# Gathers that wait for TensorE: a limit of eight groups from the thirteenth group of tiles on

## The reference

```
h = silu(einsum('td,efd->tef', x, w1))
h_mean = einsum('tef,te->ef', h, mask) / max(counts, 1)
y_mean = einsum('ef,edf->ed', h_mean, w2)
out = einsum('tk,tkd->td', routing_w, y_mean[top_idx])
```

## Time and profile before

| | us |
|---|---|
| timed runs, median of 3 | 421.34 (420.61 to 424.37) |
| profiled execution, span from first to last instruction | 501.4 |
| PE busy in the profiled execution | 397.6 |
| VectorE busy | 311.4 |
| ScalarE busy | 218.1 |
| GpSimd busy | 205.3 |

### The profile page before, as it was taken

The page is one execution under the profiler, slowest core; times in us unless marked ns, Lnnn a source line. Parts: engine busy times, 40 slices in busy tenths (PEclk is TensorE's granted clock), DMA queues, the critical chain, the costliest instruction groups (busy, mean ns, idle before and its releaser), DMA issues.

```text
span 501.4 us, 7310 instructions
## 1 busy us (share of the span) xinstructions
PE 397.6 (79%) x1929; PEld 269.9 (54%) x1930; DVE 311.4 (62%) x827; ACT 218.1 (43%) x423; POOL 205.3 (41%) x231
## 2 busy tenths in 40 slices
PE   8999999998898987554591404589987877899984
PEld 7888888886898974423440101244433433344552
DVE  3598888888788999543530101577744543577884
ACT  3334555445232666536350101456644443567320
POOL 2011111115400998757467775400066666610510
PEclk9999999998998996756587556799999788999998
DMA  6206533322209350647312111100291111100029
GB/s 182 66 1 164 139 86 109 102 80 82 81 1 262 98 140 2 193 140 212 106 57 52 54 52 43 31 0 2 54 331 47 37 47 42 47 16 1 1 73 251
DMA packets 53020, 43.68 MB, mean 87 GB/s; under 512 B 20686, under 2 KB 45980, under 8 KB 52732
## 3 DMA queue, kind: packets, MB, share of 16 engines
q1 hardware_dynamic: 44276, 32.09, 22.3%
q0 software_dynamic: 4416, 9.05, 6.5%
q10 hardware_dynamic: 4296, 2.15, 1.6%
HBM read 34.86 MB, written 8.42 MB: 86 GB/s over the span
## 4 chain that ended last, share of the span: by engine, by line
PE 47%; DVE 19%; issue 12%; another core or an unknown queue 10%; ACT 6%; POOL 3%; DVEq 2%; ACTq 0%; POOLq 0%
PE P L662 16%; PE P L935 14%; PE P L867 6%; ACT P L1265 4%; DVE BIG L1712 3%; DVE H L1828 2%; PE P L905 2%; PE P L1062 2%; PE P L697 2%; PE P L655 1%; POOL XN L597 1%; DVE arena L1504 1%; POOL arena L594 1%; PE P L688 1%
## 5 line engine op out<-in xcount | busy, mean ns | idle before, releaser
L1712 DVE TENSOR_TENSOR BIG<-BIG,P 128x512 f32 x138 | 95.0, 688 | 115.9 <-issue 75.1
L935 PE MATMUL P<-w1T,arena 128*128 x276 | 142.4, 652 | 12.0 <-DVE BIG L1712 8.7
L935 PEld LDWEIGHTS P<-w1T,arena 128*128 128x128 f32 x276 | 52.6, 209 | 67.1 <-issue 66.4
L1254 ACT COPY arena<-P 128x384 f32<-128x384 f32 (+1 forms) x48 | 22.4, 467 | 119.6 <-remote 50.4
L1265 ACT ACTIVATE P<-P 128x512 f32<-128x512 f32 x138 | 72.8, 580 | 1.6 <-PE P L935 1.5
L614 POOL DMA_INDIRECT XN<-table,arena x60 | 58.1, 968 | 30.1 <-issue 18.1
L614 POOL DMA_INDIRECT arena<-table,arena x42 | 39.7, 946 | 57.9 <-PE P L935 40.8
L557 POOL TENSOR_TENSOR rs<-ve,mhalf 123x4 f32<-123x4 f32 x16 | 17.6, 1098 | 101.9 <-DVE ve L1356 101.9
L1103 ACT ACTIVATE arena<-P 128x492 f32<-128x492 f32 x48 | 27.9, 583 | 50.6 <-PE P L662 50.5
L614 POOL DMA_INDIRECT BIG<-table,arena x36 | 34.6, 960 | 24.7 <-remote 12.4
L905 PE MATMUL P<-ident,XN 128*128 128x128 f32 x60 | 11.4, 304 | 41.6 <-issue 35.3
(11 more groups left out here) (242 smaller groups left out, 639.7 us busy)
## 6 DMA issues: line engine op xcount, KB each, us to landing
arena<-kpad SPq DMA_DIRECT2D x16, 492.0 KB, 4.0
XN<-in_L_ffn_w SPq DMA_DIRECT2D x1, 4096.0 KB
arena<-in_x SPq DMA_DIRECT2D x16, 224.0 KB
table<-XN SPq DMA_DIRECT2D x4, 896.0 KB
BIG<-table SPq DMA_DIRECT2D x1, 2048.0 KB
out<-H SPq DMA_DIRECT2D x8, 224.0 KB
out<-H ACTq DMA_DIRECT2D x8, 224.0 KB
BIG<-table SPq DMA_DIRECT2D x1, 1024.0 KB
```

The costliest lines, as they stand in the source:

```text
L935: mm = nc.tensor.matmul(bank[:, :], stat, w1T[:, bass.ds(e * FF, FF)], start=True, stop=True)
L1254: nc.scalar.copy(GTs[:, bank, 0:count * SLOT], PT[:, 0:count * SLOT]).then_inc(GT_ready, 1)
L1712: v.tensor_tensor(at, at, bank[:, :], ALU.add).then_inc(esum_step, 1)
```

## The change

A constant FREE_GROUPS = 12 takes the place of EARLY_GROUPS in the loop that issues the gathers. Groups 0 to 11 (tiles 0 to 35) do not wait for `group_mm`. Every group from the thirteenth on, g = 12 and up, waits until `group_mm` is at least g - 7, so until the transposes of group g - 8 are done. For groups 12 to 19 this wait is new; for groups 20 to 27 it takes the place of a wait for the group 20 before; for groups 28 and up it is the wait that they had. Buffers, indices, table, the other waits and all other engines stay as they are.

```diff
 EARLY_GROUPS = UNROLLED // GG
+FREE_GROUPS = 12
...
             for g, (first, count) in enumerate(GROUPS):
-                if g >= EARLY_GROUPS:
-                    pool.wait_ge(group_mm, g - (GSLOTS if g >= EARLY_GROUPS + GSLOTS else EARLY_GROUPS) + 1)
+                if g >= FREE_GROUPS:
+                    pool.wait_ge(group_mm, g - GSLOTS + 1)
                 for n in range(first, first + count):
```

## The result

The changed kernel takes 423.33 us (median of 11 runs, 422.90 to 426.46) against 421.58 us for the kernel before in the same series. The ratio is 1.005 [1.0031, 1.007], so the change costs 2.1 us [1.3, 3.0]: a real loss, and within the 1% that was called no change.

What follows compares the result with a forecast made beforehand. In a stage without stops, TensorE's products set the end, with GpSimd's slower gathers 2.4 us ahead. A 6.4 us stop makes rows 4.0 us late, less 1.7 given back: 421.3 + 2.3 = 423.6 us, range 419.5 to 428.0.

Steps and rivals of the forecast that it cites:

- The stops: Engine standstills in the first profile, 97.0 us in all; at most 16.9 us of them can be in a timed run.
- The sum: Rows 4.0 us late at the end, less 1.7 us given back: 2.3 us added to 421.3, giving 423.6 us.
- One stop, then a slide: GpSimd stands still 6.4 us before tile 36, group 12's first gather; the whole gather stream then slides by that.
- Later waits never last: After group 12 the count is always up before GpSimd needs it; closest at group 18, 285.4 against 286.1 us.
- The detour: TensorE's transposes of the routing weights at tiles 23 to 26, taken to add 4.4 us to the products.
- Who ends last before: Before the change the products set the end, tile 137's rows being there 2.4 us ahead of TensorE.
- The tail: After the last transposes, a last tile alone needs 3.1 us instead of 4.8, giving 1.7 us back.
- The landing: Time from a gather's issue until its rows arrive, taken as 2.8 us, with 1.7 kept for the range.
- The clock: TensorE's short late waits, up to 0.85 us a group from about group 36, cost no granted clock: nothing taken.
- Faster: Rival: free gathers stop the engines in timed runs too; pacing them removes 8.8 us, giving 412.5 us; chance 0.09.
- No effect: Rival: the gathers never come onto the path, so the time stays at 421.3 us; chance 0.21.
- Slower: Rival: gathers held by three wide VectorE operations lose 3.7 us, total gain in time 5.5, 426.8 us; chance 0.24.

Runs made afterwards that it cites:

- e1: The kernel before, unchanged, run again for a second profile: 421.35 us, ratio 0.9999, profiled span 419.6 us.
- e2: The kernel before with the new limit of eight groups at group 12 only: 423.52 us, ratio 1.0045.
- e3: The changed kernel with a limit of ten groups instead of eight for groups 12 to 27: 421.36 us, ratio 1.0003.
- e4: The changed kernel with a limit of six groups instead of eight for groups 12 to 27: 430.75 us, ratio 1.0232.
- e5: The kernel before with the second transposes of the routing weights behind tile 31 instead of tile 26: 421.30 us, ratio 1.0001.
- e7: The kernel before without the three gathers of group 9, whose transposes take group 0's rows: 418.21 us, ratio 0.9931.
- e10: The changed kernel with VectorE's 123x1024 operations beside gathers (one-hots, two products and sum of the weights) in quarters: 424.58 us, ratio 1.0071.
- e12: The changed kernel with only the two products and the sum of the weights on VectorE in quarters: 423.51 us, ratio 1.0053.
- e9: The kernel before with VectorE's 123x1024 operations beside gathers (one-hots, two products and sum of the weights) in quarters: 420.23 us, ratio 0.9968.

## Why the prediction was right, and where its sum was wrong

**The stops.** Right: they are in none of the later profiles. The sum had left up to 16.9 us of them in a timed run; in fact it had taken away too much. Tile 9's products come 14.4 us earlier in e1 (248.14 for 262.54), not 24.0, and from there to the last addition's end e1 takes 136.7 us (to 379.23 + 5.61), not 132.0. Between e1's span and its own time, 421.30, lie 1.7 us; the 9 to 15 us that the Trainium skill, "Runtime: NRT & Kernel Launch", section on the ~15µs preamble/postamble breakdown, gives for what surrounds a kernel are not seen here.

**One stop, then a slide.** Right as a mechanism: e2 gives the time with one wait, e3 and e4 move the stop and the time moves with it. The size was wrong, 2.4 us (and 0.5 at group 18) for 6.4. The first step that failed is the gap between tile 36 and tile 9's products, which I read as 257.21 against 262.54, 5.3 us; in e1 it is 247.02 against 248.14, 1.1 us. The disturbed execution had stretched it at both ends. TensorE's timeline in that first profile of the kernel before:

```profile
251.30 0.52 PE L905 MATMUL P<-ident,XN 128*128 128x128 f32 x3
252.03 4.53 PE L935 MATMUL P<-w1T,arena 128*128 x6 [0.21 <-issue]
```

There the first six products took 4.53 us, at a granted clock of 0.61 (252.03 to 256.40); undisturbed they take 2.84, at 1.00: 1.7 us. And tile 32 was issued 0.2 us after the first product (252.21 against 252.03), when GpSimd had stood 3.02 us there for the routing's last products on TensorE; undisturbed it comes 2.7 us after the first product (242.10 against 239.40), because GpSimd arrives later than these and does not stand: 2.5 us. Together 4.2, the difference between 5.3 and 1.1.

**Later waits never last.** Nearly right. I put group 18's count at 285.4 for a gather at 286.1. The detour was costed at 4.4 us; undisturbed, tiles 21 to 30 take 15.35 us (259.83 to 275.18) for three groups that are worth 8.72, 6.6 us more. That turns the margin of 0.7 us into 1.5 too little; the two gathers held for 1.1 us in between take most of it back, and what is left is the stop at tile 54, 0.5 us.

**Who ends last before.** Wrong: I had the rows 2.4 us ahead of the products. e1's chain, e5 and e7 show the stream ending last, with 2.4 us of TensorE's time lost to it. Two steps failed. One is the error above in another place: tile 36 comes 4.2 us later against TensorE than I read it. The longer detour (2.2 us) and the quicker landing give more than half of that back, so that at tile 137, the one that I compared, the rows would still be ahead by some 1.1 us: in e1 they land at about 376.5 (374.10 and the 2.4 of tile 134), and at e7's pace TensorE would have reached its transposes at 377.6 (e7: 247.45, tile 9's products, to 376.94; e1: from 248.14). The other step is the choice of tile 137. The wait that sets the end is that of group 44, tiles 132 to 134, three gathers earlier: from its transposes TensorE has 7.0 us of work up to those of tile 137 (369.97 to 376.94 in e7), GpSimd only 3.75. Its rows landed at 372.76 in e1, and at e7's pace TensorE would have stood there at 370.66: 2.1 us behind, not ahead.

**The tail.** Wrong too, and for the same reason: the last tile is never alone, so nothing is given back. VectorE's last additions in the changed kernel:

```profile
382.39 5.61 DVE L1713 TENSOR_TENSOR BIG<-BIG,P 128x512 f32 x7 [0.22 <-DVE BIG L1713]
```

They end at 388.00, 4.8 us after the transposes of tile 137 at 383.18, whose rows had landed by about 379.7. It is the same 4.8 us in e1 (380.02 to 384.84) and e7 (376.94 to 381.75), where the products set the end. The forecast's 3.1, and the 1.7 us that it was to save, are in no run.

**The sum.** 6.4 - 2.4 - 1.7 = 2.3 was forecast; 2.9 in the profiles' spans and 2.1 [1.3, 3.0] in the runs was measured. In the same terms the stops are 2.4 + 0.5 instead of 6.4, the lead is none instead of 2.4, and the short tail gives none instead of 1.7. That the total came out has two reasons. The wrong place of tile 36 makes the stop and the lead too long alike and drops out of their difference as long as there is a lead. The rest is luck: by the pace of the products the rows cost 5.5 us after the change and not 4.0, none of which comes back instead of 1.7, and 2.4 us of the 5.5 had been lost before the change already, where I had none.

**The landing.** Taken as 2.8, from a row of another transfer; this line on the gathers of the changed kernel shows 2.5:

```profile
DMA to landing us min/median/max: 2.4/2.5/7.8
```

**The clock.** Right to take nothing for the late waits: the granted clock is 1.00 where they lie. The changed kernel's windows over the expert stage and over its last 23 us (length, busy us by engine, then the granted clock):

```profile
239.40:387.40 148.00, 141.90 (x434) 67.94 (x434) 99.04 (x146) 92.56 (x191) 103.00 (x108) 0.99 0.24 78
...
357.00:380.00 23.00, 20.62 (x58) 8.97 (x59) 12.75 (x19) 12.21 (x26) 16.04 (x17) 1.00 0.17 52
```

It fell elsewhere: between 262 and 268 us, after TensorE had stood 0.42 and 1.25 us for VectorE at the detour, it was 0.72, in the changed kernel and in e1 alike. That is part of the detour's 6.6 us and no price of the change.

**The rivals.** Faster falls: there are no stops to take away, and the changed kernel is slower. No effect falls: 1.0031 is the lower end. Slower had a real mechanism, though not its price. VectorE's timeline of the changed kernel, one of the three operations:

```profile
263.23 1.22 DVE L1791 TENSOR_TENSOR arena<-arena 123x1024 f32<-123x1024 f32 x1
```

The gather that began 0.10 us after it took 1.94 us instead of 0.94 and ended 0.82 after the operation's end; another, begun 1.01 into such an operation, ended 0.82 after it too (259.50 + 1.03 against 258.49 + 1.22). A gather that begins ahead of the operation is not held (260.83, 0.94 us, beside the one at 260.86). So the rule of the Trainium skill, "SBUF — State Buffer", section "Who interferes with whom", that such an operation shuts GpSimd out, is borne out better here than I thought from the 0.51 of 1.22 us of the first profile. Read in the same way, that gather fits too: it ended 0.81 us after the operation (321.01 + 1.46 against 320.44 + 1.22). But e1 has the same hold (1.94 us at 263.26), so it is no price of the change. After the change what is saved on it goes into the stops (e10, e12).

**Left open:** what stopped the engines in the first profiled execution; how much of e9's gain belongs to which operations; when a gather gets through between two quarters; and how much of e10's larger loss is its routing, which ended 0.8 us later in the one execution seen.

## What to carry to other kernels

When two streams end at nearly the same time and one throttles the other, each place at which the throttle bites moves everything behind it, to the end: cost those places, and find out which stream ends last before the change. Compare the two not at the last piece but at the last one that still has a queue of work behind it (group 44 here, not tile 137). If a profiled execution is far longer than the timed runs (501 against 421 us here), the distances between engines in it are as doubtful as its length; have a second one before taking a difference of a few us from it. Idle time ahead of the waiting instruction understates what late data cost (the rows showed 0.6 us in e1, the pace of the products 2.4), so compare the pace with that of an undisturbed stretch.

## What the runs showed of the hardware

- One program had profiled executions of 501.4 and 419.6 us; the first holds some 80 us of stops that none of the other 13 profiled executions has.
- An indirect gather of 128 rows of 512 bytes takes GpSimd 0.94 us with 0.30 between two, and lands 2.5 us after its issue at the median (2.40 in e1 and 2.46 in the changed kernel for the one that TensorE waited for last).
- A gather that begins within a VectorE operation with both inputs in SBUF ends 0.82 us after that operation; with four quarters in its place, a gather that met the first ended 0.82 us after that quarter (1.01 to 1.03 us long), but two that began in the second or third (1.85 us in e9, 1.41 in e10) were held until 0.82 us after the fourth.
